# A two-layer decoder on one core: cross scores in three units, the bias product on the whole array, first operands placed in two groups of heads, new tables of steps

## The chip, the core and the metric

The kernel runs on one core of a Trainium2 chip. The metric is the device time of one execution in microseconds, as the median of several runs. The engines named here are TensorE (PE; PEld is its weight load), VectorE (DVE), ScalarE (ACT), GpSimd (POOL) and SyncE (SP), which here only issues DMAs. ScalarE issues some DMAs too.

## The reference

Four sequences of 512 tokens with 128 features go through two decoder layers, each with self-attention, cross-attention to a context of 154 tokens and a feed-forward part, with a layer norm behind each. What the change touches lies in layer 0:

```python
def _L0_attn_ref(x, W_qkv, q_scale, k_scale, W_out):     # 16 heads of 8 features
    qkv = jnp.einsum('bsd,de->bse', x, W_qkv)
    q, k, v = jnp.split(qkv, 3, axis=-1)
    q = _layernorm(q, q_scale)
    k = _layernorm(k, k_scale)
    ...
    scores = jnp.einsum('bshd,bthd->bhst', q / jnp.sqrt(Hd).astype(q.dtype), k)
    scores = jnp.where(future[None, None, :, :], jnp.finfo(scores.dtype).min, scores)
    attn = jax.nn.softmax(scores, axis=-1)
    ctx = jnp.einsum('bhst,bthd->bshd', attn, v)
    ...
def _L0_xattn_ref(q, k, v, Wq, bq, Wk, bk, Wv, bv, Wo, bo):  # 16 heads, 154 keys
    ...
def _L0_ffn_ref(inputs, gate_w, gate_b, expert_w, expert_b):  # 8 experts
    ...
    for e in range(E):
        out = out + weights[:, e:e + 1] * (x @ expert_w[e] + expert_b[e])
```

Layer 1 has linear attention, cross-attention with 8 heads of 128 features, and a gated feed-forward part of width 384.

## The kernel before

**One list of steps.** All engines walk through the same list of steps `(input, name, ...)` and do their part of each, in its order. The steps stand in streams; the string `MERGE` names letter by letter the stream whose next step follows, and `BANK_OF` gives each step that needs PSUM its bank (or pair of banks). The two strings are the tables. Semaphores join the engines: a step on TensorE waits until the earlier user of its bank is drained.

**Prelude.** For input 0: x is transposed (`x0T`), q, k and v are made in four products (`qkv`, line 1105), copied out by ScalarE (1542), VectorE takes statistics (`qk_moments`, 1786 and 1794), GpSimd the root (954, 957), q and k are normalised, transposed (`qkT`) and split into three bf16 parts each (`parts`; ScalarE 1566 and 1571, VectorE 1831 and 1840). Step `wT` transposes the context (n = 0 to 3) and the weights of the later stages (n from 4 on). Step `wM` multiplies such weights.

**Placement.** The score products run on four tiles of 64 x 64 of the array. Their operands `Q6` and `K6` hold, in every group of 8 partitions, 6 rows with the six pairs of parts of q and k; DMAs place them there from `parts` (`place`, 6 for q and 6 for k an input: SyncE in line 785, ScalarE half of those for input 0 in line 1517). The rows between hold the negative maxima.

**A turn.** For 4 of the 16 heads and 512 queries: the scores (`S`, 1149, causal mask 1131) go to VectorE, which takes the maximum of each query (`maxima`, 1868 and 1873, into `mparts`). TensorE transposes these (`mT`, 1228), ScalarE copies them to `mrows`, SyncE places them in `Q6` (806). Then the transposed scores (`ST`, 1176) come out with the maxima subtracted, ScalarE takes exponentials (`EX`, 1600), and `PV` (1219; 1203 and 1207 for the cross turns) multiplies them with the values. Self and cross turns of neighbouring inputs alternate in fours. A cross turn has four score units of 2 x 154 columns on a pair of banks.

**The rest.** Behind an input's cross turns its gates, experts, linear attention, second cross-attention and feed-forward part run, in halves of 256 tokens, between the turns of later inputs. Step `mb` (1360) multiplies the 16 gates of two blocks with the experts' biases `eb`.

The lines that name what is placed and when the first scores may begin:

```python
def placement(b, a, w, s, part):
    n = C if a and w else S
    to = (Q6, K6)[w][a][s:P:ROW_STEP, b % 2, :, 0:n]
    return to, (xkparts if w else xparts)[:, part, 0:n] if a else parts[:, w, part, :]
...
if u == g == 0:
    pe.wait_ge(cross_placed if a else qk_placed, placed_until(b))
```

## Time and profile before

| what | value |
|---|---|
| median of 3 runs | 483.26 us (483.22 to 484.2) |
| the profiled execution | 484.66 us, span 482.9 |
| PE busy | 449.9 us (93%) |
| PEld busy | 303.5 us (63%) |
| DVE busy | 381.7 us (79%) |
| ACT busy | 346.9 us (72%) |
| POOL busy | 187.2 us (39%) |

The span is the part of the execution that the profile covers; times in it count from its start. Busy shares are means over stages of different kinds, so the table of stages in the rows below says more than these. Ends of matmuls are modelled, and PE and PEld overlap.

### The profile page before, as it was taken

The page shows a single profiled execution, that of the slowest core. Times are in us where ns is not written, and L with a number is a line of the kernel's source. Part 1 is how long each engine was busy: PE and PEld are TensorE (multiplying, and loading weights), DVE is VectorE, ACT ScalarE, POOL GpSimd, SP SyncE. Part 2 cuts the span into 40 slices and gives each one's busy share as a digit, 9 for nine tenths or more (in the row PEclk, how much of TensorE's full clock was granted, in tenths as well). Part 3 has the DMA queues.
Part 4 walks back from the last instruction along what each step waited for, and adds up shares of the span by engine and source line. Part 5 has one row for each costly group of instructions (what it writes and reads, how often), then busy time and mean ns, then how long its engine had stood idle before and what let it go on. Part 6 is the DMA issues. An engine that isn't in the chain of part 4 may idle for free.

```text
span 482.9 us, 14117 instructions
## 1 busy us (share of the span) xinstructions
PE 449.9 (93%) x5296; PEld 303.5 (63%) x5296; DVE 381.7 (79%) x1083; ACT 346.9 (72%) x879; POOL 187.2 (39%) x356
## 2 busy tenths in 40 slices
PE   5767889998999999999999999999999999999995
PEld 4534446654555546656778555668774765896984
DVE  2469897898899999898698988867879687764566
ACT  1635676976868878888667788996867878869642
POOL 7284000680202364434142252335334538644532
PEclk8677999999999999999999999999999999999999
DMA  7481210034200201131100000030000000000001
GB/s 230 99 209 32 76 46 5 24 89 105 60 13 14 68 2 39 39 92 34 37 4 13 13 3 4 3 76 19 3 13 14 1 1 2 1 1 1 2 12 33
DMA packets 27191, 18.50 MB, mean 38 GB/s; under 512 B 8217, under 2 KB 26773, under 8 KB 26997
## 3 DMA queue, kind: packets, MB, share of 16 engines
q1 hardware_dynamic: 23413, 15.44, 12.1%
q10 hardware_dynamic: 3712, 2.17, 1.9%
q8 instruction: 43, 0.70, 0.6%
q14 instruction: 23, 0.19, 0.1%
HBM read 5.58 MB, written 1.05 MB: 14 GB/s over the span
## 4 chain that ended last, share of the span: by engine, by line
PE 46%; DVE 4%; ACT 2%; POOL 1%; issue 1%; POOLq 0%; DVEq 0%; ACTq 0%
PE psum L1070 6%; PE psum L1452 6%; PE psum L1429 5%; PE psum L1463 3%; PE psum L1365 3%; PE psum L1149 2%; PE psum L1474 2%; PE psum L1176 2%; PE psum L1219 2%; PE psum L1203 2%; PE psum L1454 1%; PE psum L1321 1%; PE psum L1326 1%; PE psum L1373 1%; PE psum L1207 1%
## 5 line engine op out<-in xcount | busy, mean ns | idle before, releaser
L1600 ACT ACTIVATE EX<-psum 128x1024 f32<-128x1024 f32 (+1 forms) x128 | 119.3, 975 | 7.2 <-PE psum L1131 4.2
L1873 DVE TENSOR_REDUCE mparts<-psum 128x2 f32<-128x768 f32 (+1 forms) x96 | 77.5, 862 | 3.4 <-PE psum L1131 3.0
L1868 DVE TENSOR_REDUCE mparts<-psum 128x4 f32<-128x616 f32 (+1 forms) x80 | 68.0, 877 | 4.8 <-PE psum L1149 3.6
L1028 POOL TENSOR_TENSOR GP<-REST,xrs 128x512 f32<-128x512 f32 (+1 forms) x48 | 34.6, 743 | 48.8 <-DVE xrs L2100 24.8
L1149 PE MATMUL psum<-K,Q 64*64 64x154 bf16 (+8 forms) x1024 | 48.1, 266 | 4.9 <-DVE mparts L1873 2.2
L1176 PE MATMUL psum<-Q,K 64*64 64x512 bf16 (+7 forms) x640 | 42.9, 313 | 3.4 <-DVE mparts L1873 1.5
L1689 ACT ACTIVATE REST<-psum,nxmax 128x154 f32<-128x154 f32 x96 | 36.2, 393 | 9.2 <-DVE nxmax L2090 8.2
L1149 PEld LDWEIGHTS psum<-K,Q 64*64 64x64 bf16 x1024 | 22.3, 106 | 28.0 <-issue 14.4
L1219 PE MATMUL psum<-EX,V 128*32 128x256 f32 (+3 forms) x512 | 37.8, 435 | 1.2 <-ACT EX L1600 1.2
L954 POOL TENSOR_SCALAR rstd_rest<-moments_rest 128x2 f32<-128x2 f32 x32 | 7.3, 228 | 73.2 <-DVE moments_rest L1908 72.8
L954 POOL TENSOR_SCALAR rstd_attn<-moments_attn 128x4 f32<-128x4 f32 x8 | 1.9, 238 | 82.1 <-DVE moments_attn L1908 82.1
L2090 DVE TENSOR_REDUCE nxmax<-psum 128x2 f32<-128x308 f32 x64 | 28.9, 470 | 4.6 <-PE psum L1429 4.1
L1429 PE MATMUL psum<-GP,xT 128*128 128x308 f32 x96 | 30.3, 431 | 0.1
L1176 PEld LDWEIGHTS psum<-Q,K 64*64 64x64 bf16 x640 | 15.4, 105 | 19.1 <-issue 5.6
L1219 PEld LDWEIGHTS psum<-EX,V 128*32 128x32 f32 x512 | 15.1, 109 | 18.8 <-issue 15.8
L1615 ACT COPY pvraw<-psum 128x512 f32<-128x512 f32 x16 | 9.4, 587 | 21.1 <-PE psum L1219 20.9
L1452 PE MATMUL psum<-VM,REST 128*128 128x128 f32 x192 | 23.8, 277 | 0.3 <-ACT EX L1600 0.2
L957 POOL TENSOR_TENSOR rstd_rest<-rstd_rest,power 128x2 f32<-128x2 f32 x32 | 22.9, 715 | 2.7
L1452 PEld LDWEIGHTS psum<-VM,REST 128*128 128x128 f32 x192 | 22.5, 192 | 1.1 <-issue 0.6
L1365 PE MATMUL psum<-ew,xT 128*128 128x512 f32 x48 | 22.7, 607 | 0.0
L1070 PE MATMUL psum<-ident,X 128*128 128x128 f32 x90 | 17.6, 294 | 5.1 <-DMA Y_rest<-in_ctx 3.7
L1070 PE MATMUL psum<-ident,pvraw 128*128 128x128 f32 x128 | 20.0, 279 | 1.4 <-ACT EX L1600 1.1
(344 smaller groups left out, 1151.3 us busy)
## 6 DMA issues: line engine op xcount, KB each, us to landing
Q<-xparts SPq DMA_DIRECT2D x24, 128.0 KB
Q<-parts SPq DMA_DIRECT2D x21, 128.0 KB
K<-parts SPq DMA_DIRECT2D x21, 128.0 KB
X<-in_x SPq DMA_DIRECT2D x4, 256.0 KB, 3.1
Q<-in_L_xattn_Wkv SPq DMA_DIRECT2D x1, 1024.0 KB, 7.2
K<-xkparts SPq DMA_DIRECT2D x24, 38.5 KB
out<-XB_rest SPq DMA_DIRECT2D x6, 128.0 KB, 1.8
Q<-in_L_xattn_Wq SPq DMA_DIRECT2D x1, 512.0 KB, 4.3
```

The costliest lines, as they stand in the source:

```text
L1028: last = nc.gpsimd.tensor_tensor(of.XP[:, at:at + 4 * n].rearrange("p (h c) -> p h c", h=4)[:, :, 0:c1 - c0], of.XE[:, :, c0:c1], of.xrs.r ...
L1070: last = nc.tensor.transpose(to[0:n, at:at + m], src, ident[0:m, 0:m])
L1149: last = mm(to[half, r, at:at + n], Q6[a][p, b % 2, 2 * g + jj, P * q + TILE * e:P * q + TILE * e + TILE], K6[a][p, b % 2, 2 * g + jj, 0:n ...
L1176: last = mm(to[half, r, at + q - P * k:at + S - P * k], K6[a][p, b % 2, 2 * g + jj, P * k + TILE * e:P * k + TILE * e + TILE], Q6[a][p, b ...
L1219: last = mm(to[32 * h:32 * h + 32, P * k:S], V[:, k, 4 * g + h, :], EX[:, ex_slot(b, a, g, u) + h % 2, at:at + n], start=k == PV_ORDER[0], ...
L1365: fills_(mm(fill(key), half_of(b, h).xT[2][:, P * i:P * i + P], ew[:, 4 * side:4 * side + 4, :].rearrange("p e d -> p (e d)")), key)
L1429: fills_(mm(fill(key)[:, 0:2 * C], half_of(b, h).xT[4][:, P * q:P * q + P], G[:, head:head + 2, :].rearrange("p h c -> p (h c)")), key)
L1452: mm(to, of.XPT[:, head, :], VM[:, head, :], start=head == 0, stop=False)
L1600: drains(nc.scalar.activation(dst, src, ACT.Exp), key)
L1689: last = nc.scalar.activation(of.XE[:, i, :], src[:, C * j:C * j + C], ACT.Exp, bias=of.nxmax[:, i:i + 1], accum_out=of.xsum[:, i:i + 1])
L1868: last = vec.tensor_reduce(nmax[:, :, :, q], src[:, :, 0:2 * n].rearrange("p r (j k) -> p r j k", j=2), AX.X, ALU.max, negate=True)
L1873: last = vec.tensor_reduce(nmax[:, :, jj, q], src[:, :, at:at + P * (q + 1)], AX.X, ALU.max, negate=True)
```

## The change

Four edits and new tables:

1. The scores of a cross turn come in three units of 3, 3 and 2 blocks of 154 columns instead of four of 2; VectorE takes the maxima of a whole unit in one instruction.
2. `eb` and `gT` have 128 partitions instead of 16, zero behind the first 16, so that the biases' product runs on the whole array. The gates of the last input lie in `qkn`.
3. The columns of q and k are ordered by groups of 8 heads, and each placement of the self-attention becomes two of half the partitions of `parts` (64 instead of 128). For input 0 the first group of 8 heads goes first, and the first scores wait for it alone (`first_placed`); the second group follows on SyncE behind five small loads, and is waited for at the turn g = 2. The other inputs get 24 placements instead of 12.
4. The first transposes of the context stand behind the q, k, v products of input 0, and GpSimd no longer clears all of `cT`. ScalarE issues the late loads (`late`) in step `qkT` of input 1 instead of its last `qkv`.

`MERGE` and `BANK_OF` are written anew.

```diff
-X_PIECES = [[(0, 0, q), (C, 1, q)] for q in range(NB)]
+X_COUNT = P * NB // C
+X_PIECES = [[(C * (i - first), i // NB, i % NB) for i in range(first, min(first + X_COUNT, 2 * NB))]
+            for first in range(0, 2 * NB, X_COUNT)]
...
 MERGE = (
-    "rurrrruuruuruwrrrllwllurrrrrusssssuvssssutrtstsrltstssspspttttlstprssplpsttssttstlup"
+    "rrrrrrrurwrlrllwlrrrrurruuusssssuuussuusssttttsrssvtlssppttlssttrstlssppsptstswttptl"
...
+        def half_placement(b, w, s, part, y):
+
+            return (Q6, K6)[w][0][s:P:ROW_STEP, b % 2, NQ * y:NQ * y + NQ, :], parts[
+                TILE * y:TILE * y + TILE, w, part, :]
...
-        eb = sb("eb", [2 * E, 2, D])
+        eb = sb("eb", [P, 2, D])
...
-        gT = sb("gT", [2 * E, 2, P])
+        gT = sb("gT", [P, 2, P])
...
                 if b == 0 and y:
+
+                    if w:
+                        load_early(behind)
+                        sp.wait_ge(first_zeros_ready, 1)
+                        for m in range(2):
+                            sp.dma_start(eb[E * m:E * m + E, m, :], L0_ffn_expert_b
+                                         ).then_inc(eb_loaded, 16)
+                        for of in range(2):
+                            for s, part in (*shares(of, 0), *shares(of, 1)):
+                                sp.wait_ge(part_ready[0][part], 1 + of)
+                                sp.dma_start(*half_placement(0, of, s, part, 1)
+                                             ).then_inc(qk_placed, 16)
                     return
...
                     sp.wait_ge(part_ready[0][part], 2 * b + 1 + w)
-                    sp.dma_start(*placement(b, 0, w, s, part)).then_inc(qk_placed, 16)
+                    if b == 0:
+                        sp.dma_start(*half_placement(0, w, s, part, 0)
+                                     ).then_inc(first_placed, 16)
+                    else:
+                        for of in HALVES:
+                            sp.dma_start(*half_placement(b, w, s, part, of)
+                                         ).then_inc(qk_placed, 16)
...
-            step(nc.gpsimd.memset(cT[:, :, :], 0.0))
+            step(nc.gpsimd.memset(cT[:, :, C:CP], 0.0))
...
-                if u == g == 0:
-                    pe.wait_ge(cross_placed if a else qk_placed, placed_until(b))
+                if a == b == u == g == 0:
+                    pe.wait_ge(first_placed, 16 * 2 * SLOTS)
+                elif u == 0 and g == (0 if a or b else 2):
+                    pe.wait_ge(cross_placed if a else qk_placed, placed_until(b, a))
...
-                if b == 1 and n == NB - 1:
-                    load(late)
...
+                if b == 1 and w == 0:
+                    load(late)
...
-                if len(pieces) == 2 and pieces[0][2] == pieces[1][2]:
+                if a:
+                    n, first = len(pieces), NB * pieces[0][1] + pieces[0][2]
+                    last = vec.tensor_reduce(
+                        three[:, :, 0, first:first + n],
+                        src[:, :, 0:n * C].rearrange("p r (m k) -> p r m k", m=n),
+                        AX.X, ALU.max, negate=True)
+                elif len(pieces) == 2 and pieces[0][2] == pieces[1][2]:
```

What the tables do to the order shows best in three places. First TensorE at the start of the program (X is x or the context, Y_rest its last 26 rows, Q_1 holds weights here, qkn the normalised q and k); before:

```order
L1060 MATMUL psum<-ident 128x128 x6
L1070 MATMUL psum<-ident,X 128x128 x5
L1070 MATMUL psum<-ident,Y_rest 128x26
L1060 MATMUL psum<-ident 128x128 x2
L1105 MATMUL psum<-wqkv_p,xT 128x384 x4
```

and of the change:

```order
L1089 MATMUL psum<-ident 128x128 x6
L1099 MATMUL psum<-ident,X 128x128 x4
L1089 MATMUL psum<-ident 128x128 x2
L1134 MATMUL psum<-wqkv_p,xT 128x384 x4
L1099 MATMUL psum<-ident,X 128x128
L1099 MATMUL psum<-ident,Y_rest 128x26
L1099 MATMUL psum<-ident,qkn 128x128 x8
```

The first transpose of the context (one of the five with X, and the one with Y_rest) stood ahead of the four products with `wqkv_p` and stands behind them.

Second SyncE, from the first placements to the turns of input 1 (`parts` are placements, `mrows` rows of maxima); before:

```order
L785 DMA Q_0<-parts 16x8x512 x3
L785 DMA K_0<-parts 16x8x512 x3
L806 DMA Q_0<-mrows 6x8x128
L785 DMA Q_0<-parts 16x8x512 x3
L806 DMA Q_0<-mrows 6x8x128
L785 DMA Q_0<-parts 16x8x512 x3
L806 DMA Q_0<-mrows 6x8x128
L785 DMA K_0<-parts 16x8x512 x6
L806 DMA Q_0<-mrows 6x8x128 x2
```

and of the change:

```order
L816 DMA Q_0<-parts 16x4x512 x3
L816 DMA K_0<-parts 16x4x512 x3
L786 DMA rows<-in_L_xattn_bo 128x128
L786 DMA rows<-in_L_attn_bo 128x128
L786 DMA cols<-in_L_attn_bq 128x1
L786 DMA cols<-in_L_attn_bk 128x1
L786 DMA cols<-in_L_attn_bv 128x1
L798 DMA eb<-in_L_ffn_expert_b 8x128 x2
L803 DMA Q_0<-parts 16x4x512 x6
L803 DMA K_0<-parts 16x4x512 x6
L842 DMA Q_0<-mrows 6x8x128 x2
L820 DMA Q_0<-parts 16x4x512 x12
```

Twelve placements of input 0 stand ahead of the first two rows of maxima now, and the six of input 1 that stood around the second row are twelve in one block behind it.

Third TensorE around the biases' product (`eb`) of the first half of input 1; before:

```order
L1131 MATMUL psum<-maskS,ident 64x2x64 x2
L1360 MATMUL psum<-eb,gT 128x128 x2
L1176 MATMUL psum<-Q_0,K_0 64x512 x2
```

and of the change:

```order
L1376 MATMUL psum<-gw,xT 128x8 x2
L1391 MATMUL psum<-eb,gT 128x128 x2
L1396 MATMUL psum<-ew,xT 128x512 x2
```

It stood between two tiled score units, and stands between two products on the whole array.

## Rows read from the trace of the kernel before

**Rows 1.** Stages, busy time (instructions) of each engine, granted clock, DMA share, GB/s.

```profile
6.00:8.00 2.00, 0.00 (x0) 0.00 (x0) 1.72 (x2) 0.00 (x0) 1.94 (x2) 1.00 0.77 213
10.00:16.00 6.00, 5.43 (x12) 2.81 (x11) 1.52 (x7) 2.21 (x5) 0.95 (x3) 0.59 0.95 300
24.00:31.00 7.00, 5.30 (x14) 2.36 (x12) 2.89 (x10) 3.41 (x7) 5.21 (x4) 0.67 1.01 223
32.00:60.00 28.00, 21.28 (x385) 12.33 (x389) 25.61 (x44) 14.79 (x21) 9.84 (x17) 0.88 0.30 79
60.00:228.00 168.00, 160.19 (x2403) 96.18 (x2399) 152.68 (x382) 131.99 (x279) 56.12 (x99) 1.00 0.18 46
228.00:468.00 240.00, 237.64 (x2393) 172.52 (x2391) 181.10 (x574) 183.63 (x547) 98.76 (x199) 1.00 0.04 11
```

**Rows 2.** Timeline of TensorE to 32 us: start, duration, instruction, [idle before <-releaser].

```profile
8.76 0.48 PE L1070 MATMUL psum<-ident,X 128*128 128x128 f32 x1 [3.72 <-DMA Y_rest<-in_ctx]
...
10.41 4.98 PE L1105 MATMUL psum<-wqkv_p,xT 128*128 128x384 f32 x8
...
25.38 2.93 PE L1105 MATMUL psum<-wqkv_p,xT 128*128 128x384 f32 x4 [0.99 <-ACT xT L1501]
...
31.97 0.41 PE L1149 MATMUL psum<-K,Q 64*64 64x448 bf16 x4 [1.13 <-issue]
```

**Rows 3.** Timeline of VectorE and GpSimd from 5 to 18 us.

```profile
5.45 0.44 DVE L2126 COPY wqkv_p<-REST 128x128 f32<-128x128 f32 x1
...
7.59 0.38 DVE L2129 MEMSET VX<- 128x384 f32 x1
...
10.77 0.30 POOL L895 MEMSET eb<- 16x256 f32 x1
...
15.94 0.49 DVE L1786 BATCH_NORM_STATS2 qkstats<-qkn 128x6 f32<-128x128 f32 x2 [0.45 <-ACT qkn L1542]
...
16.46 0.64 DVE L1794 BATCH_NORM_AGGREGATE qkmoments<-qkstats 128x2 f32<-128x6 f32 x8
```

**Rows 4.** Timeline of the issuing engines (SPq, ACTq) from 15 to 34 us.

```profile
15.49 1.24 SPq L771 DMA_DIRECT2D cols<-in_L_xattn_bk  x2
...
26.29 1.87 ACTq L1517 DMA_DIRECT2D K<-parts  x3
...
32.96 0.51 ACTq L1520 DMA_DIRECT2D REST<-in_L_ffn_w_down  x1
```

**Rows 5.** Issue times by line: minimum/median/maximum ns, first and last start in us.

```profile
L785 SPq DMA_DIRECT2D K<-parts x21: 542/597/610, 24.7 to 207.5; - x21
L799 SPq DMA_DIRECT2D K<-xkparts x24: 533/597/1088, 95.8 to 320.2; - x24
L831 SPq DMA_DIRECT2D eb<-in_L_ffn_expert_b x2: 286/310/334, 18.2 to 18.6; - x2
```

**Rows 6.** SyncE's timeline, and who waited for its rows of maxima (us, times).

```profile
39.57 0.85 SPq L806 DMA_DIRECT2D Q<-mrows  x1
...
57.75 3.77 SPq L785 DMA_DIRECT2D K<-parts  x6
65.61 0.77 SPq L806 DMA_DIRECT2D Q<-mrows  x1
...
  PEld psum L1176: 0.5, 2
```

**Rows 7.** Groups by form: VectorE's maxima, busy us, mean ns, idle before.

```profile
L1873 DVE TENSOR_REDUCE mparts<-psum 128x2 f32<-128x768 f32 x32 | 30.5, 952 | 1.3 <-PE psum L1131 1.1
...
L1873 DVE TENSOR_REDUCE mparts<-psum 128x2 f32<-128x256 f32 x32 | 13.4, 418 | 0.0
```

**Rows 8.** The chain that ended last: start, us, what (four matmuls each).

```profile
283.75 0.50 PE psum L1380 x4
...
298.93 0.64 PE psum L1380 x4
...
395.39 0.64 PE psum L1360 x4
```

107 lines of the change are left out of this document (60 added, 47 removed).

## The prediction

> **What bounds the kernel now.** I read the table of stages first, then TensorE's timeline of the first 32 us, then the other engines there, and last the rows of what the change touches.
>
> The table of stages [rows 1] shows three regimes. From 60 us on TensorE is the fullest, busy 160.19 of 168 us and then 237.64 of 240. From 32 to 60 us it is VectorE, busy 25.61 of 28 while TensorE leaves 6.7 us idle. Before 32 us nothing is saturated: a chain of single steps runs there. All engines follow one list of steps, in order, so an earlier start of the first scores moves everything behind it, if the list behind is as dense as before.
>
> In that prelude [rows 2] TensorE stands still for 3.72 us until the context's load lands at 8.76, because the context's first transpose (step wT 0) stands ahead of the q, k, v products. These start at 10.41, although their operands were there sooner: the last rearranging copy of their weights, the later of the two operands, ends at 5.45 + 0.44 = 5.89 [rows 3]. At the other end the first scores start at 31.97 after 1.13 us of idle without a releaser of an engine: they wait for the placement DMAs, and in 24 to 31 us the DMA engines are full (share 1.01, 223 GB/s [rows 1]).
>
> **The change part by part.**
>
> *Order in the prelude.* wT 0 goes behind the products, so these can start at 6.0, 4.4 us sooner. Do the statistics follow? Before, the aggregation began 1.07 us after the last product's end (10.41 + 4.98 = 15.39, 16.46 [rows 2, 3]). The 4.98 us are at half clock: the granted clock is 0.59 in 10 to 16 us, where it was 1.00 from 6 to 8, though TensorE did nothing there [rows 1]. These are the two levels, 2.4 and 1.2 GHz. At the upper one the products take half, 2.5 us, and end at 8.5. Then VectorE binds: its fills end at 7.59 + 0.38 = 7.97, four pairs of statistics of 0.49 us each, with 0.06 between, end near 10.2. Aggregation begins at 10.3 instead of 16.46: 6.2 us sooner. GpSimd must be free then: it ended its last fill at 10.77 + 0.30 = 11.07, and the fill of cT ahead of it shrinks from 640 elements to 24. Aggregation ends at 10.3 + 0.64 = 10.9, so GpSimd costs 0.2 us at most. If the products run at half clock throughout, the aggregation begins at 6.0 + 4.98 + 1.07 = 12.05, and the gain is 4.4. I take 6.2, since no product but the last lies past 8.0 and that one is covered by the statistics.
>
> *From there to the first scores.* Normalisation, transposes, splitting and issue are the same chain, so ScalarE's last placement issue ends at 26.29 + 1.87 - 6.2 = 22.0 [rows 4]. SyncE must be free at 22.64 - 6.2 = 16.4: before, its last load that stays ahead of the placements ended at 15.49 + 1.24 = 16.7, and two loads of rows that were ahead of it go behind, each at least the 0.31 us of a small one [rows 5], so 16.1. Half the bytes (0.77 of 1.54 MB) move in 3.5 us at 223 GB/s, less than their issue takes (6 times 0.6 us on each queue, behind the parts that become ready one by one), so the DMA no longer decides. I take 24 for its landing, 2 us behind the last issue; before, with full DMA engines, it was 31.97 - 28.16 = 3.8 at most. What decides next is ScalarE and TensorE: the second input's four products start at 25.38 - 6.2 = 19.2 and take 5 us at half clock, 24.2; then three context transposes, and their copies, which stand ahead of the first scores in the new order because the scores take a bank of one of them. With 1.3 us for these: 25.5. Gain 6.4; between 4.5 (half clock above) and 7.5 (the DMA alone decides).
>
> The Trainium skill (DMA: Bandwidth & Descriptors, Rules for kernel authors) speaks against the split: two transfers to disjoint partition halves serialise, one for all partitions is better. Here they are to serialise, the first half first. If splitting brought nothing, the first scores would start at 31.97 - 6.2 = 25.8 and the sum would lose 0.3 us; the split is worth little either way, the order is worth most.
>
> *Second halves and doubled placements.* For the first input 12 half placements follow on SyncE, 0.60 us each [rows 5], 7.2 us, ahead of the first row of maxima: SyncE is free near 31, that row is ready no sooner than 39.57 - 6.4 = 33 [rows 6]. Covered by 2 us. For the later inputs SyncE issues 24 instead of 12. The issue time does not go by bytes: placements of 512 and of 154 columns take the same 597 ns, the eight-row load 310. I take 0.60 for a half, between 0.31 and 0.60. So 7.2 us more for each of three inputs, on a queue with much idle time; what can be late is the maxima row behind a block. Before, one input's K block ends at 57.75 + 3.77 = 61.5, and the next row of maxima is issued at 65.61 [rows 6]; with 12 it ends at 65.3, just in time, but the second input's scores come next on TensorE and wait for its landing. In all of before TensorE waited for maxima rows 0.5 us, twice. I price this at 0.8 us, between 0 and 3.
>
> *Late loads on ScalarE.* Six issues of about 0.5 us [rows 4] move from a time when ScalarE had nothing else, into the first exponentials. 3 us of ScalarE, in a stage where it is busy 14.79 of 28 us [rows 1]: most is absorbed. 0.5 us, between 0 and 2.
>
> *Cross scores in three units.* VectorE's maximum costs 418 ns for 256 elements and 952 for 768 [rows 7]: 1.04 ns an element and 0.15 us fixed. The elements stay, one fixed part falls away per group of heads: 16 x 0.15 = 2.4 us of VectorE. TensorE has the same matmuls in 48 instead of 64 handovers. TensorE binds where they lie, so I take 0.3 us, between 0 and 2.4.
>
> *Biases' product.* Four matmuls with 16 rows (step mb) take 0.64 us on the chain, behind a full-array product too; four full-array ones take 0.50 behind another full step and 0.64 behind a tiled one [rows 8]. So the wider shape gains only where its neighbours are full. In the order before, six of the eight stand between tiled units; in the new one all eight have a full-array step ahead or behind. 8 x 0.14 = 1.1 us, between 0 and 1.1, all where TensorE binds. GpSimd's two added or wider fills lie in its idle time.
>
> The Trainium skill (TensorEngine Tiling (Array Packing), Key Properties) says that changing the tiling mode drains the engine. The rows agree with it. It would also speak against the new tables if they changed shapes more often: counted by steps TensorE changes 274 times, before 268, or 272 if the 16-row product counts as a shape. By that rule and the row's 0.14 us this would be 0.3 us more.
>
> *New tables behind the prelude.* By the work that stands between a step and the one that needs it (maxima to transposed scores, products to their transposes) the orders are alike: the same sequence, with steps shifted by one or two places. I price it at 0.3 us of loss, between 1 us of gain and 3 of loss.
>
> **Sum.** -6.4 - 0.3 - 1.1 + 0.8 + 0.5 + 0.3 = -6.2. The profiled execution took 484.66 us (span 482.9 and 1.8 around it), so 478.5 for such a one; the median of the timed runs is 1.4 below it, 483.26, so 477.1.
>
> **The rivals.**
> - *The shift is partly eaten.* The first scores are 6 us sooner, but VectorE or ScalarE lose 3 to 5 us by 84 us. For it: the late loads, and that VectorE has only 2.4 us of idle time in 28 there [rows 1], so what it loses it doesn't regain. Against: the same work stands there as before. 480.3 to 482.3.
> - *The new order is also denser.* In 32 to 228 us TensorE leaves 6.7 + 7.8 = 14.5 us idle [rows 1]; if a fifth to two fifths went, 3 to 6 us more: 471.1 to 474.1. For it: fewer handovers. Against: the orders are alike.
> - *Slower: SyncE's blocks.* There are six places where a block of placements grows by six issues, 3.6 us. If each of these made the row of maxima behind it, and so transposed scores, exponentials and products, late by 2 us on the mean, 12 us go: 483.3 - 6.2 - 0.8 + 12 = 488.3 (the 0.8 is what the sum holds for this already). It decides from 1.2 us a place. For it: such a block would have ended within 0.3 us of the next row. Against: 0.5 us of such waits in all [rows 6].
> - *The change does not start sooner.* The products wait for something not seen, a bank or GpSimd, or the second chain (the second input's products at half clock) is longer: gain under 1 us, 482.3 to 484.2.
>
> **How the numbers follow.** Forecast 0.62 (475 to 480.3); partly eaten 0.12; denser 0.13; slower 0.06; no start 0.07. A measurement here tells 0.2% from no change, about 1 us. The range for 8 in 10 takes the forecast's, most of the denser one and of the partly eaten one: 471.5 to 481.5. Faster 0.87, same 0.06, slower 0.07.
>
> **What would show it.** In the changed profile: the first q, k, v product near 6.0; aggregation near 10.3 and GpSimd's root near 11; the first scores at 25 to 26.5 with VectorE or ScalarE as releaser; the DMA share falling before that; mb at about 0.5 us on the chain; cross maxima of 924 elements at 1.11 us; the waits of TensorE for rows of maxima still under 2 us; the stage 228 to the end as long as before. Wrong would be: products at 8.5 or later, half clock in them, placements that push maxima out by microseconds, or a TensorE idle time behind 60 us that differs from before by more than 3 us.

## The result, and the profile after

The changed kernel takes 492.88 us (median of 4 runs, 492.31 to 493.89), the one before 483.73 on the same chip (4 runs): a ratio of 1.0192, 95% interval 1.0169 to 1.0214. The change makes the kernel 9 us slower. The forecast was 477.1, and its range ended at 481.5. The profiled span is 491.0 us against 482.9.

A span belongs to one execution, and two executions of one kernel differ. The profiled one of the kernel before (484.66 us) is 0.9 us above the median of 483.73, and its start is late: e12 below, which has the same steps up to there, has its first q, k, v product at 9.39 instead of 10.41, its first scores at 30.51 instead of 31.97 and the transpose of turn 0 at 37.59 instead of 38.95. So of each head start against the kernel before, up to 1.4 us belong to that execution, and where spans and ratios of the timed runs differ, the ratios count.

The stages of the changed kernel, as in [rows 1]: busy time (instructions) of TensorE, its weight loads, VectorE, ScalarE and GpSimd, then granted clock, DMA share, GB/s.

```profile
6.00:8.00 2.00, 2.00 (x6) 1.30 (x6) 1.72 (x2) 0.48 (x1) 1.94 (x2) 1.00 0.68 178
10.00:16.00 6.00, 1.36 (x7) 1.37 (x8) 2.35 (x15) 2.03 (x6) 3.12 (x7) 0.82 0.99 309
24.00:31.00 7.00, 5.00 (x74) 3.54 (x73) 5.92 (x18) 2.33 (x7) 6.31 (x12) 1.00 0.37 107
32.00:60.00 28.00, 20.59 (x357) 11.33 (x361) 22.48 (x38) 13.67 (x21) 4.76 (x7) 0.88 0.32 89
60.00:228.00 168.00, 155.99 (x2287) 93.07 (x2277) 145.87 (x359) 126.79 (x257) 53.64 (x94) 0.98 0.15 40
228.00:468.00 240.00, 236.45 (x2422) 168.56 (x2421) 181.41 (x560) 186.42 (x562) 99.10 (x196) 1.00 0.05 14
```

Read against [rows 1], most of the loss is not in the last stage but in the two before it. In 32 to 60 us VectorE does 3.1 us less work than before, which is what it has done ahead of them (5.92 us in 24 to 31 us, before 2.89): by 60 us the head start is used up. In 60 to 228 us it does 6.8 us less, and TensorE 4.2 us less. TensorE's timeline to 32 us says that it is not the start either:

```profile
6.03 3.28 PE L1134 MATMUL psum<-wqkv_p,xT 128*128 128x384 f32 x8
...
14.63 1.97 PE L1099 MATMUL psum<-ident,qkn 128*128 128x128 f32 x8 [5.05 <-DVE qkn L1844]
...
19.30 5.18 PE L1134 MATMUL psum<-wqkv_p,xT 128*128 128x384 f32 x8 [0.81 <-ACT xT L1532]
...
26.27 0.41 PE L1180 MATMUL psum<-K,Q 64*64 64x448 bf16 x4
```

The first scores start at 26.27, 5.7 us sooner than the 31.97 of [rows 2]. Their aggregation is at 10.38, in VectorE's timeline:

```profile
10.38 0.64 DVE L1832 BATCH_NORM_AGGREGATE qkmoments<-qkstats 128x2 f32<-128x6 f32 x8
```

To see where a head start goes, take one event that every turn has and compare its time in both traces. I use the transpose of a turn's maxima (L1228 before, L1259 after), 32 of them. These are the times in us; of the experiments below (named in their columns) they show where each gains or loses.

```
turn   before  changed   e4      e18     e11     e7      e9      e15     e5
0       38.95    33.27   36.22   34.93   38.48   36.54   33.58   33.65   35.56
1       46.57    41.88   43.87   42.92   46.38   44.39   41.00   41.55   43.24
2       55.33    53.36   52.63   51.68   55.14   58.34   53.91   52.62   56.73
4       73.49    74.29   70.79   69.83   73.29   76.48   72.83   71.64   80.96
8      113.55   118.15  110.83  109.85  115.19  117.18  114.72  113.53  121.09
10     123.80   129.42  120.91  119.93  126.06  127.64  125.34  124.82  138.86
18     201.61   209.77  198.72  197.75  205.65  205.46  205.71  205.18  218.46
31     365.57   371.86  362.61  361.60  372.95  369.31  368.15  367.38  385.77
span    482.9    491.0   480.0   478.9   489.7   486.6   487.3   486.5   502.3
```

Changed against before: 5.7 us ahead at turn 0, 2.0 at turn 2, 0.8 behind at turn 4, 4.6 behind at turn 8 and 5.6 at turn 10. So most of the loss lies in 42 to 130 us; from there to turn 31 the lag goes between 4.7 and 8.7 and ends at 6.3, and another 1.8 us are lost behind turn 31. A part of the step from turn 1 to 2 is no loss but moved work: the step `xv` of the first input (the values of the cross-attention), which the old tables have ahead of the transpose of turn 0, stands between those of turns 1 and 2 in the new ones.

```profile
44.95 1.18 DVE L2003 TENSOR_TENSOR VXR<-psum,rows 26x128 f32<-26x128 f32 x4
46.14 0.29 DVE L2006 TENSOR_TENSOR VX<-psum,rows 128x128 f32<-128x128 f32 x1
```

That is 1.5 us of VectorE. Three places in the trace of the changed kernel show how it comes about. First ScalarE:

```profile
40.67 0.34 ACTq L1556 DMA_DIRECT2D gw<-in_L_ffn_gate_w  x1
...
43.18 0.51 ACTq L1556 DMA_DIRECT2D REST<-in_L_ffn_w_down  x1
43.73 0.26 ACT L1647 COPY mrows<-psum 48x128 bf16<-48x128 bf16 x1 [1.81 <-issue]
```

The six late loads hold its queue to 43.7 us, and the copy of turn 1's maxima, whose transpose was done at 42.1, waits behind them. Then TensorE in the same microseconds:

```profile
41.88 0.22 PE L1259 MATMUL psum<-identb,mparts 128*80 128x128 bf16 x1 [1.25 <-DVE mparts L1927]
...
45.09 0.64 PE L1180 MATMUL psum<-K,Q 64*64 64x448 bf16 x4 [1.44 <-DVE mparts L1917]
...
46.24 3.17 PE L1250 MATMUL psum<-EX,V 128*32 128x512 f32 x32
```

It stands still for 1.25 and 1.44 us, the second time because two score units in a row, (0, S, 0, 2, 0) and (0, S, 0, 2, 1), have the same pair of banks in the new `BANK_OF` (pair 2), so that the second waits until VectorE has read the first. Right behind that its granted clock falls (0.72 in the mean of 44 to 50 us, where the kernel before has 1.00), and the product of the exponentials takes 3.17 us; at full clock it takes 2.36 (e18). And SyncE:

```profile
44.92 8.92 SPq L820 DMA_DIRECT2D Q<-parts  x12
...
55.38 9.05 SPq L820 DMA_DIRECT2D K<-parts  x12
64.73 10.91 SPq L842 DMA_DIRECT2D Q<-mrows  x2
```

The blocks of twelve take 8.9 and 9.1 us where a block of six took 3.77 [rows 6]. The K block ends at 64.43, and the second input's scores on TensorE wait for its landing:

```profile
65.93 0.41 PE L1180 MATMUL psum<-K,Q 64*64 64x448 bf16 x4 [2.08 <-DMA K<-parts]
```

The list of who waited for rows of maxima (us, times; PE and its weight loads PEld can wait at the same time, so the lines don't add) says it for the whole kernel, where [rows 6] has 0.5 us:

```profile
  PEld psum L1207: 4.2, 4
  PE psum L1207: 3.0, 2
  PEld psum L1180: 1.9, 3
```

And the list of what ended the idle time of VectorE ahead of its maxima has 21.4 us in two lines, where that of the kernel before has 4.0 and 3.6:

```profile
  PE psum L1160: 13.0, 20
  PE psum L1180: 8.4, 10
```

The cross maxima came as computed, 1.107 us in the median for 924 elements; in VectorE's groups by form:

```profile
L1906 DVE TENSOR_REDUCE mparts<-psum x48: 768/1107/1121, 111.2 to 369.1; 128x6 f32<-128x924 f32 x32, 128x4 f32<-128x616 f32 x16
```

The biases' product stands on the chain five times from 260 to 440 us:

```profile
275.25 0.55 PE psum L1391 x4
284.81 0.64 PE psum L1391 x4
...
369.86 0.45 PE psum L1391 x4
377.26 0.64 PE psum L1391 x4
...
408.16 0.44 PE psum L1391 x4
```

Before, it stood there five times with 0.64 to 0.69 us. Three of the five are shorter now, as forecast for full neighbours, by some 0.5 us together.

### The profile page after: what moved, and what is told of

Its sections match the earlier page's. It is cut to its first block, busy times and chain, and to the rows that moved or that the text cites. A ratio compares the mean times of both kernels' runs of the same rounds, so it can differ in the third digit from the quotient of the medians.

```text
span 491.0 us, 14152 instructions
## 1 busy us (share of the span) xinstructions
PE 451.4 (92%) x5296; PEld 303.0 (62%) x5296; DVE 382.4 (78%) x1067; ACT 346.4 (71%) x879; POOL 188.5 (38%) x357
## 3 DMA queue, kind: packets, MB, share of 16 engines
HBM read 5.58 MB, written 1.05 MB: 14 GB/s over the span
## 4 chain that ended last, share of the span: by engine, by line
PE 68%; DVE 11%; ACT 6%; SPq 5%; POOL 4%; issue 4%; DMA 2%; ACTq 1%; POOLq 0%; DVEq 0%
PE psum L1099 10%; PE psum L1483 6%; PE psum L1460 5%; PE psum L1180 5%; PE psum L1250 4%; PE psum L1396 4%; PE psum L1207 4%; PE psum L1494 4%; SPq L820 3%; PE psum L1234 3%; ACT EX L1638 3%; PE psum L1134 2%; DVE mparts L1917 2%; PE psum L1505 2%; PE psum L1278 2%
## 5 line engine op out<-in xcount | busy, mean ns | idle before, releaser
L1917 DVE TENSOR_REDUCE mparts<-psum 128x2 f32<-128x768 f32 (+1 forms) x96 | 78.1, 862 | 12.1 <-PE psum L1160 12.0
L1906 DVE TENSOR_REDUCE mparts<-psum 128x6 f32<-128x924 f32 (+1 forms) x48 | 47.5, 1004 | 8.7 <-PE psum L1180 8.4
L1057 POOL TENSOR_TENSOR GP<-REST,xrs 128x512 f32<-128x512 f32 (+1 forms) x48 | 33.1, 711 | 46.8 <-DVE xrs L2144 24.5
L1180 PEld LDWEIGHTS psum<-K,Q 64*64 64x64 bf16 x1024 | 23.0, 109 | 29.7 <-issue 12.9
L1250 PE MATMUL psum<-EX,V 128*32 128x256 f32 (+3 forms) x512 | 39.3, 448 | 0.0
L1160 PE MATMUL psum<-maskS,ident 64*64 64x128 bf16 (+2 forms) x320 | 21.4, 233 | 0.0
```

The lines of the kernel that those rows point to most:

```text
L1057: last = nc.gpsimd.tensor_tensor(of.XP[:, at:at + 4 * n].rearrange("p (h c) -> p h c", h=4)[:, :, 0:c1 - c0], of.XE[:, :, c0:c1], of.xrs.r ...
L1180: last = mm(to[half, r, at:at + n], Q6[a][p, b % 2, 2 * g + jj, P * q + TILE * e:P * q + TILE * e + TILE], K6[a][p, b % 2, 2 * g + jj, 0:n ...
L1250: last = mm(to[32 * h:32 * h + 32, P * k:S], V[:, k, 4 * g + h, :], EX[:, ex_slot(b, a, g, u) + h % 2, at:at + n], start=k == PV_ORDER[0], ...
L1906: last = vec.tensor_reduce(three[:, :, 0, first:first + n], src[:, :, 0:n * C].rearrange("p r (m k) -> p r m k", m=n), AX.X, ALU.max, nega ...
L1917: last = vec.tensor_reduce(nmax[:, :, jj, q], src[:, :, at:at + P * (q + 1)], AX.X, ALU.max, negate=True)
```

## The experiments

Each ratio is against the kernel before on the same chip, with its 95% interval; it is not the quotient of two medians and can differ from that by up to 0.2%. "Span" is that of the profiled execution (before: 482.9, changed: 491.0), 1.7 to 1.8 us less than its time.

| run | what | median, us | ratio | span |
|---|---|---|---|---|
| changed | all edits, new tables | 492.88 | 1.0192 (1.0169 to 1.0214) | 491.0 |
| e1 | changed, late loads back | 494.81 | 1.0214 (1.0181 to 1.0248) | 494.1 |
| e2 | changed, whole placements | 488.92 | 1.0087 (1.0056 to 1.0118) | 487.6 |
| e3 | changed, both | 491.63 | 1.0142 (1.0102 to 1.0182) | 490.6 |
| e4 | before, early start | 483.0 | 0.9972 (0.9956 to 0.9988) | 480.0 |
| e5 | all edits, old order | 504.71 | 1.0426 (1.0396 to 1.0455) | 502.3 |
| e6 | e5, whole placements | 491.8 | 1.0163 (1.0141 to 1.0185) | 490.2 |
| e7 | e4, late loads as changed | 488.06 | 1.0083 (1.0054 to 1.0112) | 486.6 |
| e8 | changed, late loads on SyncE | 494.94 | 1.0208 (1.0193 to 1.0223) | 493.3 |
| e9 | e8, whole placements | 486.55 | 1.0047 (1.0027 to 1.0067) | 487.3 |
| e10 | e4, late loads on SyncE | 482.92 | 0.9963 (0.9948 to 0.9978) | 481.2 |
| e11 | before, three cross units | 489.48 | 1.008 (1.0063 to 1.0097) | 489.7 |
| e12 | before, biases' product | 484.11 | 0.9998 (0.9987 to 1.001) | 482.5 |
| e14 | changed, TensorE kept busy | 492.43 | 1.0168 (1.0144 to 1.0192) | 491.4 |
| e15 | e9, TensorE kept busy | 487.99 | 1.008 (1.0056 to 1.0105) | 486.5 |
| e16 | e10, TensorE kept busy | 483.45 | 1.0001 (0.998 to 1.0022) | 481.6 |
| e17 | e9, four cross units | 519.74 | 1.074 (1.0714 to 1.0767) | 515.7 |
| e18 | e10, new prelude | 480.44 | 0.9926 (0.9909 to 0.9943) | 478.9 |
| e19 | e17, TensorE kept busy | 519.23 | 1.0739 (1.0717 to 1.076) | 517.5 |

My first theory was D: the doubled placements on SyncE. The rivals were L, ScalarE's late loads, and T, the order of the new tables.

**e1, late loads back.**

```diff
@@ step qkT of input 1 @@
-                if b == 1 and w == 0:
-                    load(late)
@@ step qkv of input 1 @@
+                if b == 1 and n == NB - 1:
+                    load(late)
```

> The changed kernel, with ScalarE's late loads put back behind the last copy of the second input's products. In the changed kernel they stand between the first two activations of the second input's parts, ScalarE issues them from 41.05 to 43.7 us, and a copy of maxima rows starts only at 43.73, with SyncE's block of twelve placements behind it. If these loads are what the changed kernel loses (theory L), the time falls by about their 2.7 us and what they push, to 489 to 490 us. If SyncE's doubled placements are (theory D), the block at 44.9 us stays as long and the time falls by less than 1 us, to 492 to 493. If the loss lies in the order of the new tables (theory T), 492 to 493 too.

None of the three: the run is 3.1 us longer in the profiled span; the ratios (1.0214 and 1.0192) can't be told apart. The first scores start at 29.21 instead of 26.27, since ScalarE issues the loads ahead of the context's copies, and what they cost at 41 us in the changed kernel is not seen to come back.

**e2, whole placements.**

```diff
-        def half_placement(b, w, s, part, y):
-            return (Q6, K6)[w][0][s:P:ROW_STEP, b % 2, NQ * y:NQ * y + NQ, :], parts[
-                TILE * y:TILE * y + TILE, w, part, :]
+        def whole_placement(b, w, s, part):
+            return (Q6, K6)[w][0][s:P:ROW_STEP, b % 2, :, :], parts[:, w, part, :]
```

> The changed kernel with edit 3 alone taken back: six placements of 128 partitions for Q and for K of each input instead of twelve of 64, with the heads in the parts' partitions as before; tables, cross units, biases' product and late loads stay changed. Theory D (the doubled placements on SyncE delay the rows of maxima between 44 and 66 us): the blocks of 8.9 and 9.1 us fall to about 4.5, the second input's K lands 6 us or more sooner, and the time falls by 4 to 8 us, to 485 to 489. Theory L (late loads): no more than 1 us of change, 492 to 493. Theory T (tables): within 2 us of the changed kernel, 491 to 494, since the blocks lie in the same places of the order.

3.4 us less in the span, 5 us (1.05%) less by the ratios. The doubled placements are about half of what the changed kernel takes over the one before: 0.87%, 4.2 us, remain. The split starts the first scores 0.3 us sooner (26.27 against 26.55); between e8 and e9 below it is 0.8 (25.63 against 26.41).

**e3, both.**

> The changed kernel with both taken back, the doubled placements and the place of the late loads. Theory D and theory L add here: 482 to 487 us if both hold, and with the earlier first scores kept it would have to be at or under 480 if nothing else costs. Theory T: 490 us or more, and what is left over 477 is the price of the tables' order with the other edits.

490.6: in the spans, e2's and e1's shifts add (-3.4 and +3.1). Theory L, that the loads' old place would give 3 us back, has fallen in this order. That the loads cost nothing where they are is not shown by this, since their old place costs the start.

**e4, the kernel before with the early start alone.** This is the forecast's main term by itself.

```diff
 MERGE = (
-    "rurrrruuruuruwrrrllwll...
+    "rrrrruuuruuruwrrrllwll...
@@ SyncE: the late early loads go behind the first placements @@
+            load_early(early)
...
+                    if w:
+                        load_early(behind)
```

> The kernel before, with only the order of the prelude changed: the fold wT 0 behind the four products of the first input, and the six loads for later layers and the experts' biases behind the first placements on SyncE. First scores should start 4.5 to 6 us sooner. If the prediction's term was right (a start that is sooner is kept to the end), 477.5 to 479.5 us. If the rows of maxima or SyncE's queue hold the stretch from 32 to 66 us whatever the start (theory B: the gain is eaten there without edit 3 as well), 481 to 484 us.

Its first scores start at 29.02, 2.95 us sooner than before, and the table of turns shows 2.7 to 3.0 us at every turn, and 2.9 in the span. In the medians it is 1.3 us (0.3%, the interval leaves out zero). The two numbers fit: e4's profiled execution (481.73 us) is the fastest of its ten, the one of the kernel before is late by up to 1.4 us, and against e12 e4's first scores are 1.5 us sooner. So with the old order a head start is kept, and "eaten whatever the order" has fallen; but what it gains is some 1.3 us, and not 2.9.

**e5 and e6, all edits in the old order.** The tables are those of e4, with the fourth cross unit of each turn left out of them; e6 has whole placements as well.

> All edits of the change (three cross units, biases' product on the whole array, doubled placements, late loads between the first exponentials), but the order and banks of the kernel before, with only the fold wT 0 behind the first products and the fourth cross unit of each turn left out of the tables. Profiled spans so far: before 482.9, changed 491.0, changed with whole placements 487.6, before with the early start 480.0. Theory T (the order of the new tables costs most of it): 478 to 483. Theory D (the doubled placements cost it by themselves): 484 to 488. Theory C (the product of the exponentials' turn at the half clock, whatever the order): 487 to 490.

> As the run above, with the whole placements of the kernel before. Its first scores should start at 26.3 to 26.5 us as in the changed kernel. Theory T: 475.5 to 478.5, the time that was forecast for the change, and 3 to 5 us under the run above if theory D holds in part (3.4 us was its share in the new order). If the early start beyond the 3 us of the run with before's order can't be kept, 480 to 482.

Both expectations of theory T fell, and by a lot: 502.3 and 490.2. With the new tables the same edits take 491.0 and 487.6, so the order is not what costs most of it, and these edits do worse in the old one. That does not clear the new tables: a part of the difference is the place of the late loads, which costs 5 us in the old order (e7), and the comparison of e9 with e18 below is the fairer one. And the placements cost 12.1 us in the old order (2.6% between the ratios). SyncE and TensorE of e5 show the mechanism at its clearest, a row of maxima behind blocks:

```profile
115.70 0.77 SPq L842 DMA_DIRECT2D Q<-mrows  x1
116.51 0.80 SPq L811 DMA_DIRECT2D Q<-VXR  x1
117.35 8.87 SPq L820 DMA_DIRECT2D Q<-parts  x12
126.27 3.78 SPq L820 DMA_DIRECT2D K<-parts  x6
...
69.88 0.64 PE L1180 MATMUL psum<-K,Q 64*64 64x448 bf16 x4 [3.24 <-DMA K<-parts]
...
132.05 0.64 PE L1207 MATMUL psum<-Q,K 64*64 64x512 bf16 x4 [5.30 <-DMA Q<-mrows]
```

The block of twelve and six holds SyncE from 117.35 to 130.05, the next row of maxima goes behind it, and TensorE waits 5.30 us for it. In the table of turns e5 loses 6.1 us against before from turn 3 (+1.4) to turn 4 (+7.5), at the K placements' landing, and 7.6 from turn 9 to 10.

**e7, e4 with the late loads in the changed kernel's place.**

```diff
-                if b == 1 and n == NB - 1:
-                    load(late)
...
+                if b == 1 and w == 0:
+                    load(late)
```

> The kernel before with the early start, and ScalarE's late loads moved to where the changed kernel has them; cross units, biases' product and placements as before. First scores started at 29.02 us with the early start alone, behind ScalarE's seven late loads; they should start 2.5 to 3 us sooner here, at 26.3, and the time should fall to 476.5 to 478 in the profiled run (480.0 without this step). If the moved loads hold up ScalarE's first exponentials as forecast (0 to 2 us), 478 to 479.5; a rival: the clock is low in other places and the whole gain is gone, 480 or more.

486.6, so 6.6 us more than e4 in the span (1.1%, 5.4 us, between the ratios), 5.2 of them at one place: turn 2 comes 14.0 us after turn 1, in e4 8.8. ScalarE and TensorE of e7:

```profile
42.95 0.34 ACTq L1524 DMA_DIRECT2D gw<-in_L_ffn_gate_w  x1
...
46.32 1.02 ACT L1604 ACTIVATE EX<-psum 128x1024 f32<-128x1024 f32 x1 [2.69 <-issue]
...
47.40 0.41 PE L1153 MATMUL psum<-K,Q 64*64 64x448 bf16 x4 [2.15 <-ACT EX L1604]
...
48.51 4.01 PE L1223 MATMUL psum<-EX,V 128*32 128x512 f32 x32 [0.39 <-ACT EX L1604]
```

The exponentials behind the six issues start at 46.32 (43.21 in e4), TensorE waits 2.15 us for their bank, and its clock falls: the product then takes 4.01 us where e4's takes 2.36. Also the start was not 26.3 as I expected but 29.54: the late loads were not what held it in this order. The transposes of q and k start at 17.02 on TensorE (14.63 in the changed kernel), behind the folds of the context and eight transposes of weights.

**e8 to e10, late loads on SyncE**, behind its placements for the first input.

```diff
+                        for dst, src in late:
+                            sp.dma_start(dst, src).then_inc(late_loaded, 16)
```

> The changed kernel with the six late loads issued by SyncE, behind its placements for the first input, instead of by ScalarE. Neither the start (26.3 us) nor ScalarE's exponentials at 41 us pay for them. Theory L2 (wherever ScalarE issues them they cost 3 us or more: behind the last copy they hold the start back, between the exponentials they leave TensorE idle near 44 us and its clock at half level at 46 to 48 us): 484 to 488 in the profiled run, against 491.0. Theory D alone (doubled placements at 44.9 and 55.4 us): 490 to 492.

> The same with the whole placements of the kernel before (487.6 in the profiled run with ScalarE's loads). If the late loads and the doubled placements are all that the changed kernel loses, 477 to 481, near the forecast; if TensorE's clock still falls to half level between 44 and 60 us, 484 or more.

> The kernel before with the early start (480.0 in the profiled run) and the late loads on SyncE. With the loads between ScalarE's exponentials it was 486.6. Theory L2: no hole at 44 us, and the exponentials no later than with the early start alone: 478.5 to 480.5. If what cost 6.6 us was that the loads' transfers fall into the stretch 43 to 50 us and not who issues them, the same as with the early start alone here too, so this run parts the issuing engine from the start only together with the first two: if it is over 484, another cause than ScalarE's queue is to be looked for.

e10 stays near e4 (481.2 and 480.0 in the span, 482.92 and 483.0 in the median), so the loads are not dear by themselves. e10 moves both who issues them and when they move data (27.89 to 30.88 us); that it is ScalarE's queue that made e7 5 us slower, and not the transfers, is read from e7's trace above. In e8 it is the other queue: with doubled placements the late loads are issued from 32.01 to 35.24, and the first row of maxima, otherwise issued at 33.82, at 35.29. e9 has neither trouble and still ends at 487.3, though this execution (489.03 us) is the slowest of its ten; by the ratio e9 is 0.47%, 2.3 us, over the kernel before. Its head start of 5.6 us at turn 1 is 1.4 at turn 2. TensorE of e9:

```profile
44.21 0.64 PE L1178 MATMUL psum<-K,Q 64*64 64x448 bf16 x4 [1.44 <-DVE mparts L1901]
...
45.36 4.49 PE L1248 MATMUL psum<-EX,V 128*32 128x512 f32 x32
```

**e11, three cross units alone, in the kernel before.**

```diff
-X_PIECES = [[(0, 0, q), (C, 1, q)] for q in range(NB)]
+X_PIECES = [[(C * (i - first), i // NB, i % NB) for i in range(first, min(first + X_COUNT, 2 * NB))]
+            for first in range(0, 2 * NB, X_COUNT)]
```

> The kernel before with the cross scores in three units alone: the fourth unit of each of the 16 cross turns is left out of the order, its pieces lie in the other three, all else as before. Forecast: 0 to 2.4 us off (480.5 to 482.9 in the profiled run). In the old order all edits with whole placements lost 4.3 us more from 180 us on than the kernel without the edits of the cross units and the biases' product; if the units cost it (three wider units of 462 columns are ready later than four narrow ones, and what waits for a turn's maxima waits longer), 485 to 488.

Slower by 6.8 us in the span and 0.8% (3.9 us) by the ratio, where I had 0.3 us off. Nothing changes up to turn 7, the last before the cross turns; 1.7 us are lost at turn 8, the rest in steps of 0.1 to 1.1 us from turn 9 to 31, nearly all at cross turns. The 1.7 us come from a row of maxima that SyncE issued at 108.02 and for which TensorE waited until 111.73; why it landed late is not shown. It may not belong to the units: e6, with the same units, does not have this wait, and e12, without them, has one of 0.95 us at 118.93. The later steps e6 does have. The largest is turn 28 to 29, 10.5 us instead of 9.45. VectorE and ScalarE there, in e11:

```profile
342.51 2.84 DVE L1870 TENSOR_REDUCE mparts<-psum 128x6 f32<-128x924 f32 x3
...
345.88 0.85 DVE L2098 TENSOR_REDUCE nxmax<-psum 128x2 f32<-128x308 f32 x2
...
346.39 0.39 ACT L1691 ACTIVATE REST<-psum,nxmax 128x154 f32<-128x154 f32 x1 [1.81 <-DVE nxmax L2098]
```

And in the kernel before:

```profile
336.88 2.21 DVE L1868 TENSOR_REDUCE mparts<-psum 128x4 f32<-128x616 f32 x3
...
339.20 0.85 DVE L2090 TENSOR_REDUCE nxmax<-psum 128x2 f32<-128x308 f32 x2
...
339.70 0.39 ACT L1689 ACTIVATE REST<-psum,nxmax 128x154 f32<-128x154 f32 x1 [0.75 <-DVE nxmax L2090]
```

Before, three of the four units stood ahead of the maxima of another stage (nxmax) and the fourth behind them. Now all three, which hold the same elements as the four, stand ahead, and the two combining steps as well: from the turn's transpose to nxmax it is 6.20 us (345.88 less 339.68) instead of 5.14 (339.20 less 334.06). ScalarE waits 1.81 instead of 0.75 us for it and TensorE behind it. These 1.06 us are the whole difference of the turn.

**e12, biases' product alone.**

> The kernel before with the biases' product alone on the whole array. Forecast for this term: 0 to 1.1 us off, 481.8 to 482.9 in the profiled run. A rival: GpSimd's clear of gT before the rows that the second input needs, and ScalarE's wait for it, put something back: 483 to 484.

482.5, and a ratio of 0.9998: no difference that can be measured. But this is the old order, where six of the eight products stand between tiled units and the prediction had no gain either; the new order was not run without the wide product.

**e14 to e16, TensorE kept busy.** 14 products that nobody reads fill its idle time (in e16 at the fourth unit of turn 0 instead).

```diff
+                if key == (0, "S", 0, 2, 1):
+                    drained(pe, (0, "mT", 0, 1))
+                    keep_busy(bank((0, "mT", 0, 1)), 10)
```

> The changed kernel with 14 idle products of 128 columns on TensorE, 4 while it waits for the second turn's maxima and 10 while it waits for the bank of the third turn's second scores (1.3 and 1.4 us idle there). Nothing reads what they write. Theory C (the clock that falls to half level at 44 to 48 us after that idle time is what loses the head start): clock 1.00 from 44 to 50 us, the product of the exponentials 2.4 us instead of 3.8, and the time down by 1.5 to 4 us, to 487 to 489.5 in the profiled run. If the clock only goes along with the wait: 490.5 to 492.

> The changed kernel with whole placements and late loads on SyncE (487.3 in the profiled run) with the same 14 idle products. Its product of the exponentials took 4.49 us at half clock, with VectorE idle 3.05 us behind it. Theory C: 2.4 us, and 483 to 485 for the kernel. If it only goes along: 487 to 488.

> The kernel before with the early start and late loads on SyncE (481.2 in the profiled run), with 14 idle products while TensorE waits 1.93 us for the bank of the first turn's fourth scores. In that kernel, as in the one before, the clock is at half level from 33 to 43 us. If the idle time there is what makes it fall, and the stretch is bound by TensorE: 477 to 479.5. If the stretch goes by VectorE's maxima (six in 4.7 us, back to back) whatever the clock: 480.5 to 481.5.

TensorE in e15:

```profile
43.25 2.50 PE L1089 MATMUL psum<-ident 128*128 128x128 f32 x20
...
46.32 2.36 PE L1251 MATMUL psum<-EX,V 128*32 128x512 f32 x32
```

The stage from 44 to 50 us of e9:

```profile
44.00:50.00 6.00, 5.79 (x56) 2.25 (x60) 3.82 (x9) 0.08 (x1) 0.00 (x0) 0.50 0.45 123
```

And of e15:

```profile
44.00:50.00 6.00, 5.95 (x108) 3.81 (x106) 4.36 (x10) 1.64 (x3) 0.00 (x0) 1.00 0.50 134
```

So here the idle time is what makes the clock fall: without it the granted clock is 1.00 instead of 0.50 and the product takes 2.36 us instead of 4.49. But the ten took 2.50 us and not the 1.4 of the gap, and with the four ahead of them they held TensorE back by 1.5 us (its next scores start at 45.67 instead of 44.21), and the time hardly moves: turn 2 comes 1.3 us sooner than in e9, the spans are 486.5 and 487.3, and the medians point the other way (ratios 1.008 and 1.0047). e14 has the clock at 1.00 in 44 to 50 us too, and the changed kernel's time (1.0168 against 1.0192, intervals overlapping). In e16 the clock is at 1.00 from 32 to 42 us where it was 0.53 in e10, and nothing is gained: 481.6 against 481.2. In that stretch VectorE is the fullest engine, busy 9.75 of 10 us in e10.

**e17 and e19, four units in the new order.** The banks of the fourth unit are the pair that was used longest ago.

> The changed kernel with whole placements and late loads on SyncE (487.3 in the profiled run), with the cross scores in four units again: the fourth stands right behind the third in the new order, in the pair of banks that was used longest ago. If three wider units cost in the new order as they did in the old (6.8 us), 481 to 485. If the new order was made for three units and only the old one suffers from them: 487 or more.

> The run with the new order and four units, with 5 idle products (some 1.2 us; the 10 of the earlier runs took 2.5 us of a gap of 1.4) before the third turn's second scores. Theory C: clock 1.00 at 44 to 50 us and 2 to 3 us less than the same kernel without them. If only the overshoot of the earlier runs held back nothing: 0 to 1 us less.

519.7 and 519.2. This says nothing on the units: both keep the head start to turn 8 (1.0 us ahead) and then lose at each cross turn, 31 and 33 us in all at turn 31, since the banks that I gave the added unit make it wait. Nor does e19 tell anything more of the clock (517.5 against 515.7). An order made for three units can't be extended in this way, and the question stays open.

**e18, the new prelude in front of the old order.** The tables up to the first turn's maxima are the new ones, from there on the old ones; late loads on SyncE, all else as before.

```diff
 MERGE = (
-    "rurrrruuruuruwrrrllwllurrrrrusssssuvssssutrtstsrltstssspspttttlstprssplpsttssttstlup"
+    "rrrrrrrurwrlrllwlrrrrurruuusssssuuuvsusssuttstsrltstssspspttttlstprssplpsttssttstlup"
```

> The kernel before, with the new tables' order up to the first turn's maxima (its scores start at about 26.4 us, 5.5 sooner) and its own order behind, late loads on SyncE, whole placements, four units, the biases' product as before. The forecast's main term by itself: if a sooner start is kept to the end, 477 to 478.5 in the profiled run and 478 to 480 as the median. If the stretch to 60 us takes back what goes beyond some 3 us: 480 to 482. If the clock falls during the second turn as in the changed kernel: 482 or more.

The best kernel of all: 480.44 us, ratio 0.9926 (0.9909 to 0.9943), 3.1 us under the one before in the medians and 3.6 by the ratio. It starts 4.9 us sooner (27.06), 3.5 against e12, and from turn 0 to the end it is 3.7 to 4.0 us ahead of the kernel before, at every turn. TensorE and VectorE of e18 where the changed kernel loses:

```profile
44.71 2.36 PE L1235 MATMUL psum<-EX,V 128*32 128x512 f32 x32 [0.41 <-ACT EX L1604]
...
44.54 4.74 DVE L1877 TENSOR_REDUCE mparts<-psum 128x2 f32<-128x1024 f32 x6
```

Six maxima back to back in 4.74 us beside a product of 2.36: in this order three score units in three different pairs of banks (6, 4, 0) stand ahead of the product.

## Why the prediction was wrong

**The start (-6.4) was right as a start and wrong as a saving of this kernel.** The forecast was 25.5 for the first scores, and they came at 26.27, within its bounds. The aggregation came at 10.38 (10.3 forecast), the products took 3.28 us (2.5 forecast), GpSimd's root started at 11.2 (11). The base was one execution, 31.97; against e12's 30.51 the start gains 4.2 us and not 5.7. What failed is the condition that I wrote down and then did not price: "an earlier start of the first scores moves everything behind it, if the list behind is as dense as before". With the old list it holds, 2.9 of 2.95 us in e4's trace and about 4 of 4.9 in e18's (in the timed runs 1.3 and 3.1 to 3.6 us, against a start that is 1.5 and 3.5 us sooner than e12's). With the new one the distance between turns 1 and 2 is 11.5 us instead of 8.8, before any cross turn has begun, of which `xv` can explain 1.5.

**New tables (+0.3, between -1 and +3).** I compared them by the work that stands between steps and called them alike. That looked at `MERGE` only. The pair of banks that two score units in a row share is in `BANK_OF`, and I had not gone through it. Shown is that it makes TensorE wait 1.44 us (both in the changed kernel and in e9) and that the idle time makes its clock fall. Shown too is that this does not explain the time by itself: e15 has the clock back and is not measurably faster. As a whole the tables are better for these edits than the old ones, by 2.6 us of span with whole placements and 11.3 us with doubled ones. But e9 and e18, which both have whole placements, late loads on SyncE and the new prelude, are 1.2% apart in their ratios, 5.9 us: that is the price of the new tables behind the prelude, the cross units and the biases' product together, for which I had -1.1 us. At least the first of it is the tables' alone, the 4.2 us of e9 from turn 1 to 2, ahead of every cross turn. So "the orders are alike", priced at 0.3 us, is the step of the prediction that failed, beside the doubled placements below; how the rest of the 5.9 us is shared was not parted.

**Doubled placements (+0.8, between 0 and 3).** 5 us by the ratios in the new order (changed against e2; 3.4 of span), 7.8 without ScalarE's loads (e8 against e9; 6.0 of span), 12.7 in the old one (12.1 of span). The step that failed is "what can be late is the maxima row behind a block": I priced one block of one input, to the 0.3 us, and took the time that TensorE waits as the whole cost. The time of one issue was right (593 ns in the median of 72, for 597 of a whole placement), but single ones (of Q) take up to 1839 ns, and a block of twelve 8.92 and 9.05 us instead of my 7.2. Such long ones are no matter of the halves: e12 has one of 1995 ns with whole placements. This was the rival "slower: SyncE's blocks", 0.06 and 488.3: the right mechanism in the old order (e5: one place 5.3 us), in the new one about half of the loss against the kernel before.

**Late loads (+0.5, between 0 and 2).** 6.6 us in the old order (e7 against e4; 1.1%, 5.4 us, between the ratios). "Most is absorbed" because ScalarE is busy 14.79 of 28 us was the error: its share is low, but what stood behind the loads on its queue were exponentials for which TensorE waits, and they came 3.1 us later. In the new order this price can't be stated: back in their old place they hold up the start by 2.9 us (e1), and on SyncE they hold up the first row of maxima (e8). With whole placements on SyncE the spans show nothing (487.3 and 487.6), the ratios 0.4%, 1.9 us (e9 against e2, intervals that just overlap).

**Cross scores in three units (-0.3, between -2.4 and 0).** VectorE saves what I computed. Alone in the old order they cost 3.9 us by the ratio and 6.8 in the span. A loss was not in my bounds, since I counted instructions and handovers: the work of the fourth unit does not vanish, it moves into the three ahead of it, and so ahead of what other stages have on VectorE. How much of this the new tables heal was not run (e17 could not tell). The turns speak for a good part: from turn 11 to 31 e11 and e6 lose 4.9 us against before, but e9 and e2 0.9 and the changed kernel 0.5.

**Biases' product (-1.1, between -1.1 and 0).** In the old order nothing, within 0.1% (e12). The matmuls themselves take 275 ns instead of 270. In the new order the chain shows some 0.5 us for the five that stand on it, within my bounds; it was not run by itself there, and 0.5 us could not be told from nothing. The 0.14 us of [rows 8] depended on the neighbours, as I had read it.

**Sum.** The pieces don't add, because each one's price depends on what else is on the queues: in the old order e6 to e5 is 12.1 us and in the new one e2 to the changed kernel 3.4. What is shown for the changed kernel, by the ratios: it is 9.3 us over the kernel before and 12.9 over e18. From it to e9, 7.0 us are the doubled placements and ScalarE's late loads, the placements alone 5.1 (against e2) or 7.8 (e8 against e9). From e9 to e18, 5.9 us are the new tables behind the prelude with the cross units and the biases' product. Where these are lost is read from e9's turns against before: 4.2 us from turn 1 to 2 (with the 1.5 of `xv` that was moved, the wait for a bank and the low clock), 2.6 from turn 2 to 8, 1.4 from there to 31 and 1.8 behind it. Which edit causes the later ones stays open.

## What to carry to other kernels

When a change gives a head start, its value is decided by the list behind it: look for the first place where two steps in a row share a buffer or a bank, and price the queue there, before counting the start as gained. Price an added issue by what stands behind it on its queue and who waits for that, never by the busy share of the engine: six loads of 0.5 us cost 5 to 7 us in one place (e7) and nothing that was measured in another (e10). Before a difference of 1 or 2 us is read from two traces, look where these executions lie among the timed ones. And build the part that you believe in by itself: the new prelude alone, on the old order, gained 3 us where the whole change lost 9.

## What the runs showed of the hardware

The fall of TensorE's clock was more frequent than I had thought, and less costly. In e9, after idle stretches of 0.99 and 1.44 us close together, the granted clock went from 1.00 to 0.50 (of the two levels, 2.4 and 1.2 GHz) and 32 products went from 2.36 to 4.49 us; with the gap filled it stayed at 1.00. Yet full clock gave nothing where VectorE was the fullest engine (e16) and no measurable time in e15. An idle product on 128 columns of f32 shows as two matmul records and took 0.25 us at the upper level, so 10 of them overfilled a gap of 1.4 us by 1.1.

An issue of a placement with half the partitions is no cheaper than a whole one. Issue times of the K placements in the changed kernel, minimum/median/maximum in ns, for the 542/597/610 of [rows 5]:

```profile
L820 SPq DMA_DIRECT2D K<-parts x36: 531/593/1716, 55.4 to 216.0; - x36
```

The issue time of these placements follows the number of transfers, not the bytes, and single issues last up to three times as long (1839 ns here, 1995 with whole placements in e12). The Trainium skill (DMA: Bandwidth & Descriptors, Rules for kernel authors) advises one transfer for all partitions instead of two to disjoint halves. The runs agree with the advice: halves start the first scores 0.3 us sooner (26.27, and 26.55 in e2) and cost 3.4 us of span or more.
